# Second attention of a four-layer block on one core: choice, query projections and packing moved, scatters and gathers exchanged

## The chip, the cores and the metric

The kernel runs on one core of one Trainium2 chip (TRN2). The metric is the time on the device in microseconds (us), the median of three runs. Engines are named as in the profile: PE is TensorE (matmuls and transposes), DVE is VectorE, ACT is ScalarE, POOL is GpSimd, SP is SyncE. They run beside each other and meet at semaphores. Indirect DMAs (gathers and scatters of rows by index) are issued by POOL, one instruction for 128 rows; plain DMAs here by SP.

## The reference, cut to what matters

The input is 16 sequences of 512 tokens with 256 features, in float32. Four layers follow each other, each on a normalised input and each added to its input:

```python
x = x + attn_a(layernorm(x), ...)   # 16 heads, global and windowed
x = x + ffn(layernorm(x), ...)      # mixture of 16 experts, 4 chosen per token
x = x + attn_b(layernorm(x), ...)   # chunks of 128: local softmax + linear state, gated
x = x + ffn(layernorm(x), ...)      # the same mixture again
```

In `attn_b`, q, k, v and gate are projections of 256 to 512 features. For each chunk of 128 tokens there is a causal softmax of q k^T times v, and a `cross` term, q times the sum of k^T v over all earlier chunks; their sum is multiplied by the gate and projected back to 256 features.

The mixture routes each token: sigmoid scores, the two best of four groups, the four best experts in these; the weights are divided by their sum and scaled. `out` is the weighted sum of the chosen experts' outputs plus a shared expert.

## The kernel before

The kernel is four phases, one after the other, each with a program of its own for every engine: `phase_a` (first attention), `phase_f` (first mixture), `phase_b` (second attention, which also finishes the first mixture and begins the second), `phase_e` (second mixture). The change is in `phase_b` alone.

**How tokens move.** Per group of 4 sequences (`BATCH`), tokens are scattered by expert into a table in DRAM (`slots`), one indirect DMA for 128 tokens and one of their four choices, so 16 (`PICKS`) a sequence. The experts' outputs lie in `made`; 16 gathers a sequence bring them back to SBUF (`yg`), where DVE adds them with their weights (`combine`, line 1953). `phase_b` does, for sequences in turn: the gathers and the combine of the first mixture; the attention; the routing of the second mixture (`groups`, `choose`, `place`, `weigh`); and the scatters of all sequences but the last four into `slots`.

**The loop of `phase_b`.** `iterations` calls a `body` of every engine for s = -2 to 16. In body s the sequence s is in its attention core, sequence s+1 in the front (its transposes and projections), s+2 in combine and normalise, s-1 in routing. A body is cut into 20 slots e = 0 to 19 (`NSLOT`); each engine goes through them in order and within a slot by the order of the `if`s, and nothing but semaphores ties the engines together. So the slot numbers are an order written out by hand, engine by engine. I call "body 7" the stretch in which s = 7.

**PE's order in a body** (names as in the code): slot 0 the scores `D` (line 2338) and front transpose T0 (2315); slot 1 T1; slot 3 the first part of the cross scores O (2350); slot 4 the rest of O, the transposes of the softmax `PT` (2358), then projection q0; slot 5 the first product with v (2370), then q1; slots 6 and 7 q2, q3; slots 8 to 15 k and v in turn; 16 to 19 the gates; the routing matmuls rT0, rT1 at 6, rL at 8, rX (the ranks, 2292) at 16, each behind the front's of its slot. A projection is six matmuls of 128x512 (lines 2268 to 2270). Each front or routing result fills a PSUM bank (`BANK`) and raises the semaphore `f_done`; the engine that empties the bank raises `f_act` or `f_dve`, and `bank_free` makes PE wait for it before the bank's next use.

**The softmax** goes from D by DVE (mask and scale 2202, maximum 2207), ACT (exp 1901), DVE (2210, 2212) to PE's transposes, and ACT copies those out (1907) before the product with v may start. The transposed input leaves PSUM twice: by ACT as `xh` (1856) and by DVE as the rest `xl` (2189). A projection waits for both.

**DVE's order**: slot 0 the mask and the maximum; 2 `scaled`; 3, 4, 6, 7 `combine`; 8 to 12 statistics and normalisation; 10 `groups` (2000 to 2033); 13 the empty of v2, a residual sum, then `choose` (2038 to 2060), on which rX waits; 15 `moments`; 17 `place` and `weigh`; and at slot 18, when s is a multiple of 4, `table` (2098 to 2117) and `pack` (2126 to 2142) for the group that is now complete. `table` works out how many tiles each expert has, `pack` turns token ranks into row numbers; a scatter of that group waits for `packed`.

**POOL's order**: slots 4 to 11 the 16 gathers for sequence s+3, a pair in front of a further wait: the pair of slot e waits for `f_done` of the front's product of that slot, and for `c_step`, the combine that reads the buffer. Slot 8 also has the residual with its bias, `xres` (1821), which waits for earlier steps of DVE and for a store. Slots 12 to 19 the 16 scatters of sequence s-5 (bodies 5 to 13; body 14 has 32 of them in slots 4 to 19, body 15 the last 16). The scatters read `staged`, which SP loads behind the store of the normalised rows.

Of the kernel before, what the change touches and what calls it, by code (L numbers as in the profile page):

```python
# [5 lines left out]
P = 128  # L6
# [70 lines left out]
BATCH = 4  # L77
# [1492 lines left out]
def phase_b(nc, shared_c, routes1, routes2, base_d, made, x_out, xn_d, slots, w_gate, bias_corr, w_exp, wexp, wh, wl, woh,  # L1570
# [47 lines left out]
    MOMENT_SLOT, RLOG_SLOT, SCALE_SLOT, GROUP_SLOT, CHOOSE_SLOT, PLACE_SLOT, TABLE_SLOT = 15, 1, 2, 10, 13, 17, 18  # L1618
    RES_SLOT = 8
    GATHER_PAIRS, LAST_SLOT = range(4, 12), (9, 12, 15, 18)  # L1620
# [14 lines left out]
    with ExitStack() as ctx:  # L1635
# [88 lines left out]
        with nc.Block() as block:  # L1724
# [63 lines left out]
            def _(pool):  # L1788
# [22 lines left out]
                def body(s, par, core, front, ahead):  # L1811
                    for e in range(NSLOT):
                        if e in GATHER_PAIRS and 2 <= s + 3 < nseq:
                            i = e - GATHER_PAIRS[0]
                            pool.wait_ge(f_done, filled(s + 1, FRONT_AT[e][0]))
                            gather(s + 3, i // 2, PAIR_OF[i % 2])
# [10 lines left out]
                        if mine and front and e >= NSLOT - 2 * TB * len(mine):  # L1827
                            i = e - (NSLOT - 2 * TB * len(mine))
                            pool.wait_ge(f_done, filled(s + 1, FRONT_AT[e][0]))
                            scatter(mine[i // (2 * TB)], i // 2 % TB, PAIR_OF[i % 2])  # L1830
# [113 lines left out]
            def _(dve):  # L1944
# [151 lines left out]
                def table(n):  # L2096
# [11 lines left out]
                    step(nc.vector.tensor_scalar(jump[:], nt[:], float(P), float(REGION), ALU.mult, ALU.subtract))  # L2108
# [11 lines left out]
                def pack(n):  # L2120

                    w = slice(n * BATCH * PICKS, (n + 1) * BATCH * PICKS)
                    shape = [P, 2 * PICKS, EXPERTS - 1]
                    for i in range(2):
                        half = slice((BATCH * n + 2 * i) * PICKS, (BATCH * n + 2 * i + 2) * PICKS)
                        step(nc.vector.tensor_tensor(past, pickf[:, half].unsqueeze(2).to_broadcast(shape),
                                                     regs0[:, 1:].unsqueeze(1).to_broadcast(shape), ALU.is_ge))
                        seen()
                        step(nc.vector.tensor_tensor(past, past, jump[:, 0:EXPERTS - 1].unsqueeze(1).to_broadcast(shape), ALU.mult))
                        seen()  # L2130
                        step(nc.vector.tensor_reduce(moved[:, 2 * i * PICKS:2 * (i + 1) * PICKS], past, AX.X, ALU.add))
                        seen()
                    step(nc.vector.tensor_tensor(posi, pickf[:, w], moved[:], ALU.add))
                    seen()

                    step(nc.vector.tensor_scalar(posb, posi, 7, STEP - 1, ALU.arith_shift_right, ALU.bitwise_and))
                    step(nc.vector.tensor_scalar(posc, posi, P - 1, 2, ALU.bitwise_and, ALU.logical_shift_left))
                    seen()
                    step(nc.vector.tensor_scalar(posi, posi, -STEP * P, None, ALU.bitwise_and))
                    step(nc.vector.tensor_tensor(posc, posc, posb, ALU.add))  # L2140
                    seen()
                    nc.vector.tensor_tensor(picks[:, w], posc, posi, ALU.add).then_inc(packed, 1)
# [54 lines left out]
                def body(s, par, core, front, ahead):  # L2197
                    for e in range(NSLOT):
# [53 lines left out]
                        if s >= 1 and e == TABLE_SLOT and s % BATCH == 0:  # L2252
                            table(s // BATCH - 1)
# [587 lines left out]
```

## Time and profile before

| | us |
|---|---|
| median of 3 runs (3324.78 to 3342.89) | 3330.68 |
| the profiled execution's own time | 3329.18 |
| its span, first to last instruction | 3327.4 |
| PE busy | 2854.6 (86%) |
| DVE busy | 2212.1 (66%) |
| POOL busy | 1408.1 (42%) |
| ACT busy | 1480.5 (44%) |

The span lies 1.8 us under the profiled execution's time, and that 1.5 us under the median. In the page's strip of 40 slices `phase_b` is roughly slices 21 to 33 (from about 1738 to 2738 us). Busy time of PE is modelled from the starts of pipelined matmuls; what counts is whether PE waits, and at which clock it runs (PEclk, a share of full speed).

### The profile page before, as it was taken

How to read it: one execution, taken by the hardware profiler on the slowest of the kernel's cores; microseconds unless marked ns; L12 is line 12 of the kernel's file. 1: busy time of each engine (PE TensorE's matmuls, PEld its weight loads, DVE VectorE, ACT ScalarE, POOL GpSimd, SP SyncE). 2: the span in 40 equal slices, each digit the busy share in tenths (PEclk: the TensorE clock that was granted, in tenths of full speed). 3: DMA queues.
4: the chain of work that ended last, by engine and by line, in shares of the span. 5: the costliest groups of instructions: out<-in, count | busy, mean ns of one | idle time of the engine just before them, and what ended most of it. 6: DMA issues, size and time to landing. Idle time of an engine off the chain costs nothing. (4 is left out here: it accounts for less than half of the span.)

```text
span 3327.4 us, 59305 instructions
## 1 busy us (share of the span) xinstructions
PE 2854.6 (86%) x17728; PEld 2175.3 (65%) x17728; DVE 2212.1 (66%) x5557; ACT 1480.5 (44%) x3002; POOL 1408.1 (42%) x1606
## 2 busy tenths in 40 slices
PE   7999899899996769888979999889888938999982
PEld 4556556556564438777867777667666728788861
DVE  8878777877883867863546677657656554476653
ACT  3444455454453225555754343333333316666640
POOL 1332332332332265555125323545554524555555
PEclk9999999999997879999999999999999969999996
DMA  1121121121113246677762222333332238788874
GB/s 67 59 71 53 47 85 46 53 85 46 52 71 108 84 150 232 223 244 265 261 210 87 67 73 68 114 97 95 112 101 75 103 128 278 271 297 304 304 252 127
DMA packets 206294, 454.65 MB, mean 137 GB/s; under 512 B 28304, under 2 KB 119568, under 8 KB 204944
## 3 DMA queue, kind: packets, MB, share of 16 engines
q1 hardware_dynamic: 156816, 316.37, 27.7%
q0 software_dynamic: 49152, 134.28, 12.4%
q8 instruction: 162, 2.65, 0.3%
q14 instruction: 164, 1.34, 0.1%
HBM read 215.15 MB, written 234.88 MB: 135 GB/s over the span
## 5 line engine op out<-in xcount | busy, mean ns | idle before, releaser
L370 POOL TENSOR_SCALAR_AFFINE_SELECT a_pt<-a_pt 128x512 f32<-128x512 f32 (+1 forms) x320 | 178.9, 559 | 666.8 <-ACT a_pt L470 666.2
L470 ACT ACTIVATE a_pt<-a_S 128x384 f32<-128x384 f32 (+3 forms) x640 | 254.7, 452 | 265.4 <-PE a_S L768 262.1
L1035 POOL DMA_INDIRECT slots<-f_xn,k_picks x256 | 258.2, 1009 | 262.5 <-DVE k_picks L1378 112.8
L1793 POOL DMA_INDIRECT k_yg<-made,k_picks x224 | 225.9, 1008 | 337.0 <-DVE k_xin L1953 202.1
L2550 POOL DMA_INDIRECT f_yg<-made,k_picks x256 | 250.3, 978 | 196.9 <-issue 69.4
L618 DVE TENSOR_REDUCE a_mx<-a_FB 128x2 f32<-128x384 f32 (+4 forms) x512 | 275.8, 591 | 27.4 <-PE a_FB L743 16.2
L740 PE MATMUL a_FB<-a_kb,a_qb 128*128 128x192 bf16 (+4 forms) x1024 | 205.1, 266 | 59.5 <-DVE a_mx L618 52.0
L1807 POOL DMA_INDIRECT slots<-b_staged,k_picks x160 | 158.7, 992 | 106.6 <-issue 42.1
L781 PE MATMUL a_PV<-a_pt,a_vv 128*32 128x192 f32 (+4 forms) x2048 | 198.0, 370 | 2.7 <-POOL a_pt L377 2.6
L768 PE MATMUL a_S<-a_qs,a_ks 97*128 97x384 f32 (+3 forms) x640 | 178.4, 361 | 15.5 <-issue 15.2
L740 PEld LDWEIGHTS a_FB<-a_kb,a_qb 128*128 128x128 bf16 x1024 | 101.7, 100 | 136.3 <-DVE a_mx L618 88.2
L1524 PE MATMUL f_Z<-f_xe,f_wt 128*128 128x128 f32 x1280 | 161.4, 281 | 16.8 <-issue 9.1
L2595 ACT COPY f_wt<-f_wexp 128x512 f32 x240 | 144.8, 626 | 50.2 <-issue 26.3
L1524 PEld LDWEIGHTS f_Z<-f_xe,f_wt 128*128 128x128 f32 x1280 | 153.4, 196 | 20.1 <-issue 19.9
L2743 PE MATMUL f_Z<-f_xe,f_wt 128*128 128x128 f32 x1280 | 157.7, 277 | 5.2 <-ACT f_r L2608 4.6
L571 DVE TENSOR_SCALAR a_qb<-a_qh,a_headmask 128x512 bf16<-128x512 f32 x256 | 159.8, 691 | 0.0
L1143 ACT COPY f_wt<-f_wexp 128x512 f32 x240 | 145.1, 622 | 26.4 <-issue 23.1
L2743 PEld LDWEIGHTS f_Z<-f_xe,f_wt 128*128 128x128 f32 x1280 | 150.7, 193 | 6.6 <-issue 6.4
L2675 DVE SCALAR_TENSOR_TENSOR f_cb<-f_yg,k_wall,f_cb 128x256 f32<-128x256 f32 x256 | 123.9, 485 | 45.6 <-DMA f_yg<-made,k_picks 26.3
L2753 PE MATMUL f_Y<-f_wt,f_ge 128*128 128x256 f32 x640 | 151.5, 380 | 2.0 <-ACT f_ye L2614 1.1
L1534 PE MATMUL f_Y<-f_wt,f_ge 128*128 128x256 f32 x640 | 152.2, 381 | 1.1 <-DVE f_ye L1404 1.1
L2370 PE MATMUL b_PV<-b_st,b_v 128*128 128x512 f32 (+3 forms) x512 | 151.9, 440 | 0.9 <-ACT b_st L1907 0.9
(415 smaller groups left out, 7577.3 us busy)
## 6 DMA issues: line engine op xcount, KB each, us to landing
f_xg<-slots SPq DMA_DIRECT2D x160, 512.0 KB
made<-f_ye SPq DMA_DIRECT2D x160, 512.0 KB
slots<-a_zeros SPq DMA_DIRECT2D x16, 2560.0 KB, 9.2
a_xin<-in_x SPq DMA_DIRECT2D x16, 512.0 KB, 10.1
x_after_a<-a_xres SPq DMA_DIRECT2D x16, 512.0 KB, 2.9
f_xin<-x_after_a SPq DMA_DIRECT2D x16, 512.0 KB
f_wexp<-in_w_exp SPq DMA_DIRECT2D x8, 1024.0 KB, 13.1
bases<-f_xin SPq DMA_DIRECT2D x16, 512.0 KB, 4.5
```

Of the source, the lines that this page charges most:

```text
L370: ins = nc.gpsimd.affine_select(out=v[:, :, 0:P], in_=v[:, :, 0:P], compare_op=ALU.is_ge, fill=0.0, base=0, pattern=[[0, nh], [1, P]], cha ...
L470: nc.scalar.activation(pt[:, u % 4, b * w:(b + 1) * w], S[:, s_bank[2 * u + b], 0:w], ACT.Exp).then_inc(e_done, 1)
L571: ins = nc.vector.tensor_scalar(qb16[:, h, :], qh[:, t, :].bitcast(F32), headmask[:, h % HT:h % HT + 1], None, ALU.mult)
L618: nc.vector.tensor_reduce(mx[:, heads[0]:heads[0] + nh, qb], src[:, 0:nh * n].rearrange("p (h c) -> p h c", c=n), AX.X, ALU.max).then_inc( ...
L740: pe.matmul(o, qb16[:, h, qb * P:(qb + 1) * P], kb16[:, h // HT, k0:k0 + n], start=True, stop=(h < GLOBAL))
L768: ins = pe.matmul(S[:, s_bank[i], 0:nh * n], ks[0:ONES + 1, h // 2, kb * P:(kb + 1) * P], qs[0:ONES + 1, h:h + nh, kb * P:kb * P + n], sta ...
L781: ins = pe.matmul(PV[r:r + VW, kb * P:kb * P + n], vv[:, par, kb, h, :], pt[:, u % 4, j * n:(j + 1) * n], start=(kb == 0), stop=(kb == TB ...
L1035: nc.gpsimd.indirect_dma_start(out=slots[s // BATCH][:, :], out_offset=bass.IndirectOffsetOnAxis(ap=picks[:, i:i + 1], axis=0), in_=xn[:, ...
L1524: ins = pe.matmul(Z[:, b * P:(b + 1) * P], wt[:, v % WT, b, k * P:(k + 1) * P], xe[:, v % 2, k, b * P:(b + 1) * P], start=(k == 0), stop=( ...
L1793: nc.gpsimd.indirect_dma_start(out=yg[:, b, k, :], out_offset=None, in_=made[s // BATCH][:, :], in_offset=bass.IndirectOffsetOnAxis(ap=rou ...
L2550: nc.gpsimd.indirect_dma_start(out=yg[:, b, k, :], out_offset=None, in_=made[s // BATCH][:, :], in_offset=bass.IndirectOffsetOnAxis(ap=pic ...
L2743: ins = pe.matmul(Z[:, b * P:(b + 1) * P], wt[:, v % WT, b, k * P:(k + 1) * P], xe[:, v % 2, k, b * P:(b + 1) * P], start=(k == 0), stop=( ...
```

## The change

Five edits, all in `phase_b`:

1. `FRONT_SLOT`: T1 goes from slot 1 to slot 0, q0 from 4 to 3, q1 from 5 to 3, k, v and gates stay. On PE q0 and q1 now stand behind the first part of O and ahead of its rest and of `PT`; on ACT and DVE the emptying of T1 comes ahead of exp and of the softmax's scaling.
2. `choose` goes from slot 13 to slot 12, ahead of v2's emptying and of the residual sum.
3. `table` and `pack` are split. At slot 18 of body 4n: `jumps` (the first steps of `table`) and `pack` of one sequence. At slot 15 of body 4n+1: `pack` of one and then of two sequences. At slot 19 of that body: the rest of `table`. For the last group all of it stands at the end of body 16.
4. The scatters take slots 4 to 11, the gathers slots 12 to 19 (body 14 keeps its 32 scatters in slots 4 to 19; body 15 its order).
5. The waits that go with these: a pair now waits for the last front product up to its slot (`front_by`), a scatter for its own part of the packing.

```diff
-    FRONT_SLOT = (0, 1, 4, 5, 6, 7, 8, 9, 10, 11, 12, 13, 14, 15, 16, 17, 18, 19)
+    FRONT_SLOT = (0, 0, 3, 3, 6, 7, 8, 9, 10, 11, 12, 13, 14, 15, 16, 17, 18, 19)
+    def front_by(e):
+        return max(i for i in range(NF) if FRONT_SLOT[i] <= e)
-    ... GROUP_SLOT, CHOOSE_SLOT, PLACE_SLOT, TABLE_SLOT = 15, 1, 2, 10, 13, 17, 18
+    ... GROUP_SLOT, CHOOSE_SLOT, PLACE_SLOT, TABLE_SLOT, PACK_SLOT, REST_SLOT = 15, 1, 2, 10, 12, 17, 18, 15, 19
-    GATHER_PAIRS, LAST_SLOT = range(4, 12), (9, 12, 15, 18)
+    GATHER_PAIRS, SCATTER_AT, LAST_SLOT = range(12, 20), 4, (9, 12, 15, 18)
...
-                        pool.wait_ge(packed, s // BATCH + 1)
+                        pool.wait_ge(packed, 2 * (s // BATCH) + 1 + (s % BATCH > 0))
...
-                            pool.wait_ge(f_done, filled(s + 1, FRONT_AT[e][0]))
+                            pool.wait_ge(f_done, filled(s + 1, front_by(e)))
                             gather(s + 3, i // 2, PAIR_OF[i % 2])
...
-                        if mine and front and e >= NSLOT - 2 * TB * len(mine):
-                            i = e - (NSLOT - 2 * TB * len(mine))
+                        if mine and front and SCATTER_AT <= e < SCATTER_AT + 2 * TB * len(mine):
+                            i = e - SCATTER_AT
...
-                def table(n):
+                def jumps(n):
                     dve.wait_ge(f_dve, emptied(USE_NO[BATCH * (n + 1) - 1, "rX"]))
...
+                    step(nc.vector.tensor_scalar(jump[:], nt[:], float(P), float(REGION), ALU.mult, ALU.subtract))
+                    seen()
+
+                def table(n):
                     step(nc.vector.tensor_tensor(tmp16, tri16[:], ...))
...
-                def pack(n):
+                def pack(s, count, last=True):
+                    m = count * PICKS
+                    w = slice(s * PICKS, s * PICKS + m)
...                  # the same nine steps, on m columns, once for each call
...
                         if s >= 1 and e == TABLE_SLOT and s % BATCH == 0:
+                            jumps(s // BATCH - 1)
+                            pack(s - BATCH, 1)
+                        if s > BATCH and e == PACK_SLOT and s % BATCH == 1:
+                            pack(s - BATCH, 1, False)
+                            pack(s - BATCH + 1, 2)
+                        if s > BATCH and e == REST_SLOT and s % BATCH == 1:
                             table(s // BATCH - 1)
-                            pack(s // BATCH - 1)
+                        if s == nseq and e == NSLOT - 1:
+                            pack(s - BATCH + 1, 1, False)
+                            pack(s - BATCH + 2, 2)
+                            table(NG - 1)
```

## Rows read from the trace of the kernel before

**Rows 1.** Busy time by body: stretch, length, busy by engine, PEclk, DMA share, GB/s
```profile
1775.63:1824.93 49.30, 48.10 (x230) 37.65 (x229) 27.57 (x64) 18.71 (x39) 30.11 (x28) 1.00 0.35 105
1929.61:1981.99 52.38, 50.82 (x262) 40.33 (x261) 36.53 (x115) 20.49 (x44) 18.82 (x17) 1.00 0.24 72
2034.38:2098.40 64.02, 54.70 (x261) 42.99 (x260) 47.47 (x142) 20.58 (x44) 27.41 (x26) 0.92 0.27 86
2161.58:2224.46 62.88, 55.76 (x261) 43.30 (x260) 36.69 (x114) 20.58 (x44) 33.36 (x33) 0.92 0.31 98
2472.57:2537.10 64.53, 56.24 (x262) 43.93 (x260) 37.64 (x120) 20.53 (x44) 35.37 (x34) 0.89 0.32 101
2537.10:2596.45 59.35, 53.81 (x261) 41.26 (x260) 44.10 (x120) 19.00 (x42) 17.36 (x16) 0.97 0.17 58
2596.45:2658.02 61.57, 53.31 (x261) 41.22 (x260) 29.98 (x89) 21.04 (x44) 36.20 (x36) 0.98 0.31 109
```

**Rows 2.** PE's waits, bodies 2 to 4: total us, times, longest
```profile
PE b_PV L2292 <- issue: 3.6, 3, 1.2
```

**Rows 3.** PE's waits, bodies 6 to 11
```profile
PE b_PV L2292 <- issue: 16.7, 6, 3.3
```

**Rows 4.** Timeline, DVE, bodies 3, 7 and 0: start, length, instruction, [idle before, releaser]
```profile
1933.38 0.69 DVE L2202 SCALAR_TENSOR_TENSOR b_sm<-b_DB,b_maskc 128x512 f32<-128x512 f32 x1 [2.36 <-PE b_DB L2338]
...
2171.22 0.69 DVE L2202 SCALAR_TENSOR_TENSOR b_sm<-b_DB,b_maskc 128x512 f32<-128x512 f32 x1 [11.58 <-remote]
...
1782.67 0.69 DVE L2202 SCALAR_TENSOR_TENSOR b_sm<-b_DB,b_maskc 128x512 f32<-128x512 f32 x1 [11.74 <-remote]
```

**Rows 5.** Timeline, PE, starts of bodies 7 and 5
```profile
2161.58 3.73 PE L2338 MATMUL b_DB<-b_kT,b_qT 128*128 128x128 f32 x32
...
2175.31 1.12 PE L2358 MATMUL b_DB<-k_ident,b_sm 128*128 128x128 f32 x4 [3.12 <-DVE b_sm L2212]
...
2050.01 1.11 PE L2358 MATMUL b_DB<-k_ident,b_sm 128*128 128x128 f32 x4 [5.83 <-DVE b_sm L2212]
```

**Rows 6.** Timeline, POOL, end of body 7, start of body 8; then body 0
```profile
2211.20 1.01 POOL L1807 DMA_INDIRECT slots<-b_staged,k_picks  x1 [0.30 <-issue]
...
2218.17 0.97 POOL L1807 DMA_INDIRECT slots<-b_staged,k_picks  x1 [2.09 <-remote]
...
2232.20 0.97 POOL L1807 DMA_INDIRECT slots<-b_staged,k_picks  x1 [0.31 <-issue]
...
1779.71 0.95 POOL L1793 DMA_INDIRECT k_yg<-made,k_picks  x1 [0.30 <-issue]
```

**Rows 7.** Timeline, POOL and ACT, first mixture, with gathers, then without
```profile
1688.28 0.96 POOL L1070 DMA_INDIRECT k_yg<-made,k_picks  x1 [0.30 <-issue]
...
1690.21 0.60 ACT L1156 ACTIVATE f_r<-f_Z 128x512 f32<-128x512 f32 x1 [2.83 <-remote]
...
1708.01 0.60 ACT L1156 ACTIVATE f_r<-f_Z 128x512 f32<-128x512 f32 x1
```

**Rows 8.** Timeline, DVE, table and pack at the start of body 5
```profile
2035.71 0.17 DVE L2098 TENSOR_TENSOR b_nt<-b_cnt,k_regs 128x16 f32<-128x16 f32 x1
...
2044.84 0.22 DVE L2133 TENSOR_TENSOR b_raw<-k_pickf,b_moved 128x64 int32<-128x64 f32 x1
...
2045.93 0.68 DVE L2202 SCALAR_TENSOR_TENSOR b_sm<-b_DB,b_maskc 128x512 f32<-128x512 f32 x1
```

**Rows 9.** Timeline, POOL and DVE in body 13, then DVE in body 3
```profile
2553.52 2.44 POOL L1821 TENSOR_TENSOR b_xres<-k_xin,b_bo 128x1024 f32<-128x1024 f32 x1 [7.95 <-DVE b_rxn L1993]
...
2553.26 5.97 DVE L1953 SCALAR_TENSOR_TENSOR k_xin<-k_yg,k_wall,k_xin 128x256 f32<-128x256 f32 x8
...
1939.80 2.04 DVE L1953 SCALAR_TENSOR_TENSOR k_xin<-k_yg,k_wall,k_xin 128x256 f32<-128x256 f32 x4
```

**Rows 10.** Timeline, ACT in body 3: the softmax's transposes copied out
```profile
1939.89 0.79 ACT L1907 COPY b_st<-b_DB 128x128 f32<-128x128 f32 x4
```

**Rows 11.** Timeline, DVE, first instruction of the last phase
```profile
2739.13 0.43 DVE L2647 COPY f_wt<-f_wexp 128x512 f32 x1 [1.03 <-PEq L1724]
```

More of the change, by code:

```diff
@@ L1617, in phase_b @@
     C_SLOT = (3, 4, 6, 7)
-    MOMENT_SLOT, RLOG_SLOT, SCALE_SLOT, GROUP_SLOT, CHOOSE_SLOT, PLACE_SLOT, TABLE_SLOT = 15, 1, 2, 10, 13, 17, 18
+    MOMENT_SLOT, RLOG_SLOT, SCALE_SLOT, GROUP_SLOT, CHOOSE_SLOT, PLACE_SLOT, TABLE_SLOT, PACK_SLOT, REST_SLOT = 15, 1, 2, 10, 12, 17, 18, 15, 19
     RES_SLOT = 8
-    GATHER_PAIRS, LAST_SLOT = range(4, 12), (9, 12, 15, 18)
+    GATHER_PAIRS, SCATTER_AT, LAST_SLOT = range(12, 20), 4, (9, 12, 15, 18)
     PAIR_OF = (range(0, 2), range(2, TOP_K))
@@ L1826, in body @@
                             scatter(mine[0], LAST_SLOT.index(e), range(TOP_K))
-                        if mine and front and e >= NSLOT - 2 * TB * len(mine):
-                            i = e - (NSLOT - 2 * TB * len(mine))
-                            pool.wait_ge(f_done, filled(s + 1, FRONT_AT[e][0]))
+                        if mine and front and SCATTER_AT <= e < SCATTER_AT + 2 * TB * len(mine):
+                            i = e - SCATTER_AT
+                            pool.wait_ge(f_done, filled(s + 1, front_by(e)))
                             scatter(mine[i // (2 * TB)], i // 2 % TB, PAIR_OF[i % 2])
@@ L2118, in table @@
                                             ).then_inc(table_done, 1)
-                def pack(n):
[L2122 to L2133, printed above, removed]
+                def pack(s, count, last=True):
+                    m = count * PICKS
+                    w = slice(s * PICKS, s * PICKS + m)
+                    shape = [P, m, EXPERTS - 1]
+                    over, far = past[:, 0:m], moved[:, 0:m]
+                    pi, pb, pc = posi[:, 0:m], posb[:, 0:m], posc[:, 0:m]
+                    step(nc.vector.tensor_tensor(over, pickf[:, w].unsqueeze(2).to_broadcast(shape),
+                                                 regs0[:, 1:].unsqueeze(1).to_broadcast(shape), ALU.is_ge))
@@ L2134, in pack @@
                     seen()
-                    step(nc.vector.tensor_scalar(posb, posi, 7, STEP - 1, ALU.arith_shift_right, ALU.bitwise_and))
-                    step(nc.vector.tensor_scalar(posc, posi, P - 1, 2, ALU.bitwise_and, ALU.logical_shift_left))
+                    step(nc.vector.tensor_tensor(over, over, jump[:, 0:EXPERTS - 1].unsqueeze(1).to_broadcast(shape), ALU.mult))
                     seen()
-                    step(nc.vector.tensor_scalar(posi, posi, -STEP * P, None, ALU.bitwise_and))
@@ L2140, in pack @@
-                    step(nc.vector.tensor_tensor(posc, posc, posb, ALU.add))
+                    step(nc.vector.tensor_reduce(far, over, AX.X, ALU.add))
                     seen()
-                    nc.vector.tensor_tensor(picks[:, w], posc, posi, ALU.add).then_inc(packed, 1)
+                    step(nc.vector.tensor_tensor(pi, pickf[:, w], far, ALU.add))
+                    seen()
+                    step(nc.vector.tensor_scalar(pb, pi, 7, STEP - 1, ALU.arith_shift_right, ALU.bitwise_and))
@@ new lines, in pack @@
+                    step(nc.vector.tensor_scalar(pc, pi, P - 1, 2, ALU.bitwise_and, ALU.logical_shift_left))
+                    seen()
+                    step(nc.vector.tensor_scalar(pi, pi, -STEP * P, None, ALU.bitwise_and))
+                    step(nc.vector.tensor_tensor(pc, pc, pb, ALU.add))
+                    seen()
+                    ins = nc.vector.tensor_tensor(picks[:, w], pc, pi, ALU.add)
+                    if last:
+                        ins.then_inc(packed, 1)
+                    else:
+                        step(ins)
```

1 line of the change is left out of this document (removed).

## The prediction

> **What bounds the kernel now.** I read the page's strip first (PE busy nearly throughout `phase_b`), then the busy time by body. PE bounds the phase: in body 3 it is busy 50.82 of 52.38 us at full clock, while DVE has 36.53 and POOL 18.82 [rows 1]. There are two kinds of body. Bodies 1 to 4, which have gathers and no scatters, take 52.3 to 52.4 us each; the eight bodies 5 to 12 take 61.6 to 64.5 (62.8 in the mean), at a granted clock of 0.89 to 0.93 [rows 1]. So what is to be explained is 10 us times eight. PE's waits come next: in bodies 2 to 4 the only one of size is the ranks' matmul rX, 1.2 us a body [rows 2]; in bodies 6 to 11 it is 2.8 a body [rows 3].
>
> Then the start of a body. In body 7 PE computes D in 3.73 us, to 2165.31 [rows 5], yet DVE takes it up at 2171.22, after 11.58 us of idleness, released by "remote" [rows 4]. So the signal was 5.9 us late. In body 3 D starts at 1929.61 [rows 1], so ends near 1933.3, and DVE takes it at 1933.38 [rows 4]: no delay. What differs is on POOL. In body 7 the scatters of slots 12 to 19 can't keep up with PE: one every 0.97 + 0.31 = 1.28 us, 16 of them 20.5 us, and in slots 12 to 19 of a clean body only some 12 us are left; the last of body 7 ends at 2233.17, 8.7 us into body 8 [rows 6]. I read: while POOL issues an unbroken train of indirect DMAs, PE's completion signals reach the others late, and they come 1 to 2 us after it stops. Scatters are not needed for it. In body 0, before any scatter, the gathers of the start run to 1780.66 [rows 6]; D began at 1775.63 [rows 1], so was done near 1779.4, and DVE gets it at 1782.67 [rows 4], 3.3 us late and 2.0 after the last gather. In the first mixture the last of a run of gathers ends at 1689.24, ACT gets PE's bank at 1690.21 after 2.83 idle ("remote"), where without gathers it does not wait [rows 7].
>
> When the signal comes late, PE has only T0, T1 and the first of O, then waits (3.12 us before PT in body 7 [rows 5]), and a stretch at the lower of its two clock levels follows. Body 13, whose gathers are gone and which still starts behind body 12's train and has its own in slots 12 to 19, takes 59.35 [rows 1].
>
> **Edit 4, scatters and gathers exchanged (the main term).** The train in the last slots is the same length whichever kind it is: a gather takes 0.95 and 0.30 [rows 6], 16 make 20.0 us. From now on it stands there in each of the bodies -1 to 12, not only 5 to 13.
> - Bodies 1 to 4 (four): each now starts behind a train and ends in one, as body 13 did: 59.35 - 52.38 = +7.0 each. In body 13 another cost comes with it: `xres` is no longer held up by gathers before it; it runs for 2.44 us at 2553.52, and DVE's combines, eight in 5.97 us, stretch from the 4 in 2.04 of body 3 [rows 9] (0.75 against 0.51 each). That moves into bodies 1 to 4 also, as slots 4 to 11 are empty on POOL there; it is in the 7.0.
> - Bounds of this term. Below: nothing, if gathers hold nothing back (0). Above: 62.8 - 52.4 = 10.4 each, the difference of a body with both. I take 7.0, since body 13 has exactly one train of 16.
> - Body 0: it starts 3.3 us late behind gathers in slots 4 to 11 already [rows 4, 6]; with them in slots 12 to 19 they end later, and it also gets a train of its own at its end. Bounds 0 and 7.0; I take half, +3.5.
> - Bodies 5 to 12: 32 indirect DMAs before and after, 41 of 63 us of POOL's queue; the late train stays, only of the other kind. Scatters in slots 4 to 11 then are paced by PE's products, as gathers were in body 3, where nothing waited. 0. Bounds: -10.4 each (gathers harmless, the rival below) and +2.
> - Body 13: starts behind a train as before, its own scatters move ahead. Body 14 no longer starts behind one (61.57 before [rows 1]), but its 36 POOL instructions remain. Together -2, bounds 0 and -9.
>
> The Trainium skill ("DMA: Bandwidth & Descriptors", section "Anatomy of one DMA — SWDGE (gpsimd) path") says that a DMA's signal waits until its write is confirmed, and that this lasts longest where the write goes to HBM. A scatter writes HBM, a gather writes SBUF, so by that rule the exchange would take the heavier kind out of the critical end. Whether it holds PE's signals back is not on that page; the rows of body 0 and of the first mixture show gathers doing so. By the rule bodies 1 to 4 would cost less and bodies 5 to 12 gain, in the extreme as in rival A; by the rows neither.
>
> The page "SBUF — State Buffer" (section "SBUF: two separate sides") of the Trainium skill calls the port pair of DVE and GpSimd an exclusive lock, held for a whole instruction. That agrees with the combines beside `xres` [rows 9]; it would add to bodies 1 to 4 what the body-13 comparison already holds.
>
> **Edit 1, T1, q0 and q1 forward.** PE has six matmuls more twice, some 2.8 us, between the first O and PT. In a body whose D is late this could fill the wait before PT (3.12 [rows 5]), but the filling needs xl, which DVE writes at the start, and PT then stands behind q0 and q1 when DVE is done. After PT the first product with v must wait for ACT's copies, 0.79 us [rows 10] plus their signal, where q0 stood between them before. So +0.9 us in a clean body, and in one with a late D I take 1.2 (bounds -2.5, the wait filled, and +2). Bodies 1 to 4 and 6 to 12: eleven times 1.2 = +13.2.
>
> **Edit 2, choose one slot earlier.** It goes ahead of v2's emptying. The wait at rX, 1.2 us a clean body [rows 2] and 2.8 in the others [rows 3], should go. But v2's bank is then emptied later by the length of choose, and its next use waits for that; with a train at the end the releases come late anyway, and the wait passes to another line. I count 0 for all bodies (bounds -2.8, the wait gone and nothing in its place, and +1, a later bank).
>
> **Edit 3, table and pack split.** In body 5 both stood ahead of the mask: from 2035.71 to about 2045.9, 10.2 us [rows 8], and PE waited 5.83 us for the softmax [rows 5]. That wait goes, but what then is late is D itself: in body 7 the mask comes 9.6 us after the start, in body 5 it came 2045.93 - 2034.38 = 11.6 [rows 4, 8]. Gain 2 us in bodies 5 and 9, and 13's start, against some 10 us of packing now in slots 15 and 19 of the same bodies; DVE is busy 47.47 of 64.02 there [rows 1], so much is covered, yet v's and the gates' banks wait behind it. I call it 0, bounds -4 and +3 for each of the three. At the phase's end it is exposed: DVE alone works until 2738.11, 1.03 us before the next phase's first instruction [rows 11]. The last group is cut in three calls with nine steps each where there were twelve in all, 15 more instructions of about 0.2 us [rows 8]: +3, nothing hides it.
>
> **Edit 5, the waits.** A pair in slots 12 to 19 waits for the same product as before. The scatter of slot 4 waits for packing done a body earlier. Behind it on POOL stands `xres`, and behind that the gathers, whose first combine is in slot 3 of the next body. 0. In body -1 T1 and q0 reach for weights a little earlier: +1 (bounds 0 and 3).
>
> **Sum.** 28.0 (bodies 1 to 4) + 3.5 (body 0) - 2 + 13.2 + 3 + 1 = +46.7 on 3329.18: 3375.9. The profiled execution is 1.5 under the median, so 3377. Its own range, with 4 to 10 us for the main term and 0 to 2 for edit 1: 3350 to 3405.
>
> **Rivals.**
> A. Gathers, even in a long train, hold back nothing that matters, and scatters in slots 4 to 11 neither. For it: body 14 has scatters in slots 4 to 11 and a clock of 0.98 [rows 1]; the gathers of bodies 1 to 4 cost nothing. Against it: body 0 and the first mixture [rows 6, 7]. Then bodies 5 to 12 fall from 62.8 to about 52.8, 8 x -10 = -80; body 13 -6, body 14 -1; bodies 1 to 4 0; the tail +3; the packing +3. About -81: 3250. Chance 0.18.
> B. Gathers hold signals back half as much (1.5 to 3.3 us [rows 4, 7] against 5.9): bodies 1 to 4 4 x 3.5 = +14, body 0 +2, bodies 5 to 12 8 x -3.5 = -28, edit 1 +7, tail +3. About -2: 3329, from 3300 to 3350. Chance 0.22.
> C. As forecast, and more: packing in slots 15 and 19 delays the emptying of v and gates, and xl is not ready for q0. Decides where DVE's lead falls under 2 us. Another +2.5 in each of 14 bodies, +35: 3412. Chance 0.10.
> The forecast: 0.50.
>
> **How the numbers follow.** A measurement here can tell about 0.5% (17 us) from no change. Slower by more: the forecast nearly whole, C, and some of B: 0.58. Within 0.5%: 0.17, mostly B. Faster: A, some of B and of unseen gains from edits 2 and 3: 0.25. The range leaves out A's lower half and the top of C: 3270 to 3408; the likeliest case's own is 3350 to 3405.
>
> **What would show it.** Right: bodies 1 to 4 at 58 to 62 us, with DVE's mask released by "remote" 4 to 6 us after D's end, and gathers running 7 to 9 us into the next body; bodies 5 to 12 still over 61 at a clock of 0.9; no wait at line 2292 in bodies 1 to 4; a new wait at line 2370 for ACT's copies; the last phase beginning 3 us later after PE's last product. Wrong: the mask in body 7 taken up at D's end although a train of gathers still runs (A), or bodies 1 to 4 unchanged at 52.4. If the sum is right and bodies 5 to 12 have got shorter while others got longer by as much more, the mechanism is not the one I gave.

## The result and the profile after

The changed kernel takes 3410.15 us (median of 4 runs, 3405.24 to 3417.21), the kernel before 3328.36 (4 runs): a ratio of 1.024, 95% interval 1.0216 to 1.0265. It is 82 us slower (80 by the ratio); forecast was slower, at 3377, with a range to 3408. The profiled execution took 3405.24 us, its span is 3403.3 against 3327.4.

The stretches of six bodies in the changed kernel (length, busy time of PE, PEld, DVE, ACT and POOL with counts, granted clock, DMA share, GB/s), bodies 0, 3, 5, 7, 13 and 14, which answer to [rows 1]:

```profile
1774.36:1837.11 62.75, 50.05 (x230) 39.08 (x229) 26.17 (x64) 18.18 (x38) 21.06 (x22) 0.89 0.19 59
1959.66:2021.22 61.56, 54.24 (x262) 42.25 (x260) 38.45 (x114) 20.34 (x44) 17.71 (x18) 0.94 0.20 61
2082.98:2150.71 67.73, 55.85 (x262) 43.69 (x260) 44.50 (x144) 21.73 (x46) 35.33 (x35) 0.90 0.33 103
2213.32:2278.23 64.91, 55.51 (x262) 41.73 (x261) 36.84 (x115) 19.91 (x44) 34.20 (x34) 0.95 0.31 98
2601.71:2662.57 60.86, 54.85 (x261) 42.01 (x260) 37.59 (x116) 20.69 (x44) 25.44 (x24) 0.94 0.24 78
2662.57:2730.11 67.54, 54.81 (x261) 42.37 (x260) 34.78 (x108) 19.93 (x42) 28.33 (x27) 0.95 0.24 80
```

Body 3 went from 52.38 to 61.56 with the same work on PE. Every body length, read off in the same way from the starts of D (us):

| body | 0 | 1-4, mean | 5 | 6-12, mean | 13 | 14 | last, to phase_e |
|---|---|---|---|---|---|---|---|
| before | 49.3 | 52.4 | 64.0 | 62.7 | 59.4 | 61.6 | 81.1 |
| changed | 62.7 | 61.5 | 67.7 | 64.4 | 60.9 | 67.5 | 84.0 |
| difference, all | +13.4 | +36.4 | +3.7 | +12.3 | +1.5 | +6.0 | +2.9 |

They sum to 76.2, close to the difference of the spans (75.9). Half of it lies in bodies 1 to 4.

PE's waits in the whole phase of the changed kernel (what it waited for: us, times, longest):

```profile
PE b_Y L2289 <- DVE b_xl L2201: 45.3, 11, 11.8
PE b_PV L2289 <- ACT b_kT L1868: 25.7, 9, 3.1
PE b_Y L2336 <- issue: 20.4, 30, 1.1
PE b_PV L2391 <- ACT b_st L1911: 14.0, 16, 0.9
PE b_DB L2359 <- issue: 12.7, 18, 1.8
...
PE b_PV L2313 <- DVE b_chosen L2064: 6.9, 1, 6.9
```

The ranks' wait (31.6 us in this view of before) has gone but for the 6.9 of the last body. In its place q0 (line 2289) waits 45.3 us for `xl`, k3's bank 25.7 for ACT, and the product with v (2391) 16 times 0.87 us for ACT's copies.

Body 0 is the plainest case. The timelines of DVE, ACT, POOL and PE of the changed kernel there (start, length, instruction, idle before and releaser):

```profile
1787.13 0.69 DVE L2214 SCALAR_TENSOR_TENSOR b_sm<-b_DB,b_maskc 128x512 f32<-128x512 f32 x1 [15.73 <-remote]
```
```profile
1791.32 1.07 ACT L1860 CAST b_xh<-b_Y 128x512 fp32r<-128x512 f32 x2 [14.77 <-remote]
```
```profile
1787.69 0.95 POOL L1797 DMA_INDIRECT k_yg<-made,k_picks  x1 [0.30 <-issue]
1788.65 2.36 POOL L1825 TENSOR_TENSOR b_xres<-k_xin,b_bo 128x1024 f32<-128x1024 f32 x1
```
```profile
1774.36 3.73 PE L2359 MATMUL b_DB<-b_kT,b_qT 128*128 128x128 f32 x32
1777.93 1.04 PE L2336 MATMUL b_Y<-k_ident,b_xn 128*128 128x128 f32 x8
1778.80 2.75 PE L2371 MATMUL b_PV<-b_qT,b_kT 128*128 128x384 f32 x8
1793.38 0.77 PE L2289 MATMUL b_Y<-b_xh,b_wl 128*128 128x512 f32 x1 [11.82 <-DVE b_xl L2201]
...
1798.30 2.78 PE L2371 MATMUL b_PV<-b_qT,b_kT 128*128 128x256 f32 x16
```

PE has D ready at 1778.1 and both transposes at 1779.0. DVE gets the first 9.0 us later, while the gathers still run; ACT gets the second 12.3 us later, after the last of the gathers (1787.69). All this time POOL did nothing but start a gather every 1.26 us. And the 2.78 us of the rest of O, which before filled such a wait, stand at 1798.30, behind q0 and q1.

Body 3, POOL and PE, shows a second thing:

```profile
1960.49 0.95 POOL L1797 DMA_INDIRECT k_yg<-made,k_picks  x1 [0.30 <-issue]
1963.67 0.95 POOL L1797 DMA_INDIRECT k_yg<-made,k_picks  x1 [2.23 <-remote]
...
1969.95 0.95 POOL L1797 DMA_INDIRECT k_yg<-made,k_picks  x1 [0.30 <-issue]
```
```profile
1961.21 0.37 PE L2359 MATMUL b_DB<-b_kT,b_qT 128*128 128x128 f32 x1 [0.44 <-issue]
1962.61 0.27 PE L2359 MATMUL b_DB<-b_kT,b_qT 128*128 128x128 f32 x1 [1.03 <-issue]
...
1973.70 0.77 PE L2289 MATMUL b_Y<-b_xh,b_wl 128*128 128x512 f32 x1 [4.21 <-DVE b_xl L2201]
```

POOL's own wait for PE's last gate product, which PE finished by 1959.8, ended at 1963.67, 2.2 us after the train had stopped for it; so the train throttles itself once. And within D, a run of matmuls that wait for nobody, PE stopped three times, for 0.4 to 1.0 us.

Body 14 is long for another reason. Its signals are on time: ACT takes the front's transpose 4.2 us after the start, as in an undisturbed body. But DVE comes to the mask 6.9 us after D is done without having been idle, because the packing and the rest of the table, which edit 3 put at slots 15 and 19 of body 13, are worked off right in front of it:

```profile
2673.06 0.20 DVE L2124 TENSOR_SCALAR k_wofi<-b_et 128x80 int32<-128x80 f32 x1
2673.18 0.68 DVE L2214 SCALAR_TENSOR_TENSOR b_sm<-b_DB,b_maskc 128x512 f32<-128x512 f32 x1
```

The phase's end, DVE: the next phase starts 84.0 us after the last D, 2.9 later than before (81.1), as the forecast's 3 had it [rows 11]:

```profile
2814.14 0.43 DVE L2668 COPY f_wt<-f_wexp 128x512 f32 x1 [1.38 <-issue]
```

### The profile page after: what moved, and what is told of

Its sections match the earlier page's. It is cut to its first block and busy times, and to the rows that moved or that the text cites. A ratio compares the mean times of both kernels' runs of the same rounds, so it can differ in the third digit from the quotient of the medians.

```text
span 3403.3 us, 59365 instructions
## 1 busy us (share of the span) xinstructions
PE 2883.1 (85%) x17728; PEld 2189.5 (64%) x17728; DVE 2224.3 (65%) x5617; ACT 1480.7 (44%) x3002; POOL 1398.0 (41%) x1606
## 5 line engine op out<-in xcount | busy, mean ns | idle before, releaser
L2571 POOL DMA_INDIRECT f_yg<-made,k_picks x256 | 249.3, 974 | 195.6 <-issue 67.7
L1797 POOL DMA_INDIRECT k_yg<-made,k_picks x224 | 217.7, 972 | 245.0 <-PE b_FB L2291 159.6
L740 PE MATMUL a_FB<-a_kb,a_qb 128*128 128x192 bf16 (+4 forms) x1024 | 205.3, 266 | 59.6 <-DVE a_mx L618 52.2
## 6 DMA issues: line engine op xcount, KB each, us to landing
f_wexp<-in_w_exp SPq DMA_DIRECT2D x8, 1024.0 KB, 12.1
```

The costliest lines, as they stand in the source:

```text
L740: pe.matmul(o, qb16[:, h, qb * P:(qb + 1) * P], kb16[:, h // HT, k0:k0 + n], start=True, stop=(h < GLOBAL))
L1797: nc.gpsimd.indirect_dma_start(out=yg[:, b, k, :], out_offset=None, in_=made[s // BATCH][:, :], in_offset=bass.IndirectOffsetOnAxis(ap=rou ...
L2571: nc.gpsimd.indirect_dma_start(out=yg[:, b, k, :], out_offset=None, in_=made[s // BATCH][:, :], in_offset=bass.IndirectOffsetOnAxis(ap=pic ...
```

## The experiments

In each experiment "Measured" gives first the ratio to the kernel before, run on the same chip, with its 95% interval, and then what the kernel takes over it (the ratio less 1, times 3330 us). The profiles give a second measure, from one execution of each kernel: the length of `phase_b` from the first D to the next phase's first instruction, 963.5 us before. The rest of the program, which no run changed, took 2359.9 to 2380.6 us in these profiles, so part of a difference of whole times is not the edit's. Both, in us against before:

| | by the ratio | `phase_b` alone |
|---|---|---|
| the changed kernel | +80 | +76.3 |
| 1, the exchange alone | +36 | +31.6 |
| 2, all but the exchange | +23 | +18.1 |
| 3, the front alone | +47 | +34.1 |
| 4, choose and packing alone | -18 | -9.9 |
| 5, scatters spread | -38 | -51.2 |
| 6, thin gathers | +55 | +56.5 |
| 7, a train in mid-body | +41 | +54.6 |
| 8, the exchange, paced | +11 | +5.2 |
| 9, the changed kernel, paced | +26 | +30.4 |
| 10, without the front; with T1 alone | +36; +40 | +47.9; +43.5 |
| 11, staged rows earlier | +82 | +73.0 |
| 12, in the order of the text | -66, -22, -44, -57 | -54.6, -27.8, -54.5, -56.2 |

**1. The exchange alone** (edits 4 and 5).

```diff
-    GATHER_PAIRS, LAST_SLOT = range(4, 12), (9, 12, 15, 18)
+    GATHER_PAIRS, SCATTER_AT, LAST_SLOT = range(12, 20), 4, (9, 12, 15, 18)
```

> The kernel before with the exchange alone: scatters in slots 4 to 11, gathers in 12 to 19. Theory (a long unbroken train of indirect DMAs at the end of a body holds PE's completion signals back, whichever kind it is): bodies 1 to 4 go from 52.4 to 59-61 us, body 0 from 49 to 58-62, bodies 5 to 12 stay within 2 us of before, in all +40 to +60 us. Rival (the projections put forward are the main cost, PE now waits at q0 for xl, and the exchange alone costs little): under +25 us. Rival (gathers in a train are harmless): bodies 5 to 12 near 53, the kernel 50 us or more faster than before.

Measured: 1.0108 (1.005 to 1.0167), +36 us. Body 0 58.0, bodies 1 to 4 59.8 in the mean (+7.4 each), body 5 68.4, bodies 6 to 12 62.0 (before 62.7), body 14 57.3. The theory's body lengths came out, but for body 5 (+4.4); its total is just under what was expected. Neither rival: gathers in the last slots cost as much as scatters there, as bodies 5 to 12 hardly changed when the kinds changed places.

**2. All but the exchange.**

```diff
-    GATHER_PAIRS, SCATTER_AT, LAST_SLOT = range(12, 20), 4, (9, 12, 15, 18)
+    GATHER_PAIRS, LAST_SLOT = range(4, 12), (9, 12, 15, 18)      # scatters in 12 to 19
```

> The changed kernel with the exchange undone (gathers in slots 4 to 11, scatters in 12 to 19), all other edits kept. Theory: bodies 1 to 4 back to 52 to 53.5 us, the kernel +5 to +25 us over before. Rival (the projections put forward are the main cost): +50 us or more.

Measured: 1.007 (1.0044 to 1.0097), +23 us; bodies 1 to 4 at 52.2.

**3. T1, q0 and q1 forward, alone.**

```diff
-    FRONT_SLOT = (0, 1, 4, 5, 6, ...
+    FRONT_SLOT = (0, 0, 3, 3, 6, ...
```

> The kernel before with T1, q0 and q1 forward and nothing else. Theory: about +0.9 us in bodies 1 to 4 (PE waits 0.9 at the product with v for ACT's copy) and -1 to +2 in bodies 5 to 12, in all 0 to +20 us. Rival (main cost): +40 us or more.

Measured: 1.0142 (1.0101 to 1.0184), +47 us. The expectation failed, and the rival's number came. Bodies 1 to 4 are 53.5 (+1.1 each, as forecast), but body 0 is +7.4, bodies 5 to 12 +2.6 each and body 14 +5.4. PE's waits in bodies 5 to 11 of this kernel:

```profile
PE b_PV L2296 <- issue: 20.4, 7, 4.0
PE b_Y L2272 <- DVE b_xl L2193: 20.3, 6, 7.1
...
PE b_PV L2374 <- ACT b_st L1911: 2.6, 3, 0.9
```

Line 2272 is q0's. Before, PE waited 12.1 us in these bodies for the softmax ahead of PT, and never at q0. In body 7 the rest of O changed its place; first the kernel before, where all of O is done ahead of PT's wait [rows 5], then this one:

```profile
2166.03 4.69 PE L2350 MATMUL b_PV<-b_qT,b_kT 128*128 128x384 f32 x17
2171.16 1.04 PE L2350 MATMUL b_PV<-b_qT,b_kT 128*128 128x128 f32 x7 [0.44 <-issue]
```
```profile
2195.73 0.77 PE L2272 MATMUL b_Y<-b_xh,b_wl 128*128 128x512 f32 x1 [3.09 <-DVE b_xl L2193]
...
2200.12 2.78 PE L2354 MATMUL b_PV<-b_qT,b_kT 128*128 128x256 f32 x16
```

**4. Choose and packing, alone** (edits 2 and 3).

> The kernel before with choose at slot 12 and table and pack split, nothing else. From the two kernels with the front moved (+43 us with it alone, +24 with these two added) they are worth -19 us. If they add up: -15 to -25 us against before, with bodies 1 to 4 at 51 to 51.5 us. Rival (they only help behind the moved projections): within 5 us of before.

Measured: 0.9945 (0.9925 to 0.9964), -18 us, inside the expectation (-10 in `phase_b` of its one profile). Bodies 1 to 4 are 51.04 (the ranks' 1.2 us and a little more), and body 5 falls from 64.0 to 52.1, at full clock:

```profile
2036.14:2088.23 52.09, 51.02 (x261) 40.23 (x260) 39.18 (x127) 19.09 (x42) 24.49 (x24) 1.00 0.31 90
```

Bodies 6 to 12 gained nothing (62.9): there PE itself now stops again and again within D, 60 times and 41.0 us in the phase, with waits for nothing that the profile shows.

**5. Scatters spread.** The same 32 indirect DMAs in a body, in another place.

```diff
+    SINGLE = (5, 7, 9, 11) + tuple(range(12, 20))
+                        old = SCATTERS.get(s - 1, ())
+                        if len(old) == 1 and front and e < 4:
+                            pool.wait_ge(f_done, filled(s + 1, front_by(e)))
+                            scatter(old[0], TB - 1, (e,))
+                        if len(mine) == 1 and front and e in SINGLE:
+                            ...
+                            scatter(mine[0], i // TOP_K, (i % TOP_K,))
```

> The kernel before with the scatters of bodies 5 to 13 spread so that no long train forms: one each in slots 5, 7, 9, 11 and 12 to 19, the last four in slots 0 to 3 of the next body; the gathers stay. The same 32 indirect DMAs a body. Theory (the unbroken train is what costs): bodies 5 to 12 from 62.8 to 53-57 us, in all -50 to -80 us. Rival (the mere number of indirect DMAs or their traffic costs the 10 us a body): bodies 5 to 12 stay over 61, in all within 10 us of before.

Measured: 0.9885 (0.984 to 0.9931), -38 us. Bodies 6 to 12 fall from 62.7 to 57.1 in the mean, three of them to 55.8. Body 7, against 62.88 at a clock of 0.92 [rows 1]:

```profile
2153.02:2208.86 55.84, 52.38 (x261) 41.39 (x260) 36.59 (x114) 20.48 (x44) 34.14 (x34) 0.97 0.36 113
```

In bodies 6 to 12, all but 9, DVE takes the mask up at D's end again. Body 5 stays at 64.7: there the block of table and packing ahead of the mask takes over. The number of indirect DMAs is not what costs.

**6. Thin gathers.** The exchange alone, with an eighth of the bytes.

```diff
-                            out=yg[:, b, k, :], out_offset=None, ...
+                            out=yg[:, b, k, 0:32], out_offset=None, ...
```

> The kernel with the exchange alone, but each gather of this phase brings 32 of the 256 numbers of a row (the rest of the combine reads what lay there). As many gathers, an eighth of their bytes. If POOL's issuing of the train holds the signals: bodies 1 to 4 stay at 59 to 60 us. If the traffic of the train does: they fall to 52 to 55 us.

Measured: 1.0164 (1.0131 to 1.0197) on a chip where the kernel before took 3351; bodies 1 to 4 at 60.7, where the full gathers gave 59.8. Body 3 of each, first thin, then full:

```profile
1957.69:2019.22 61.53, 55.37 (x262) 42.84 (x261) 38.19 (x114) 20.05 (x44) 18.21 (x18) 0.94 0.11 30
```
```profile
1946.31:2006.11 59.80, 54.01 (x261) 42.30 (x260) 38.32 (x114) 20.15 (x44) 17.95 (x18) 0.94 0.21 62
```

30 GB/s against 62, and no gain. It is not the bytes. (The kernel leaves seven eighths of each gathered row out.)

**7. A train in the middle of the body.** The kernel before, with the gathers of bodies 1 to 4 unbroken from slot 8 on.

```diff
+                        if e == GATHER_PAIRS[4] and 1 <= s <= 4:
+                            pool.wait_ge(f_done, filled(s + 1, FRONT_AT[e][0]))
+                            for i in range(2 * TB):
+                                gather(s + 3, i // 2, PAIR_OF[i % 2])
```

> The kernel before, with the 16 gathers of bodies 1 to 4 in one unbroken train from slot 8 on, where they stood in pairs in slots 4 to 11; nothing is at the end of the body. Theory (the unbroken train costs, wherever it stands): signals of PE in slots 9 to 16 come over 2 us late and bodies 1 to 4 go from 52.4 to 55-60 us. Rival (only a train over the start of the next body costs, since D is short of cover there): under 53.5 us.

Measured: 1.0123 (1.0089 to 1.0156), +41 us; bodies 1 to 4 at 61.8 to 64.7, more than either side expected, though D's signal is on time there. POOL and ACT in body 3:

```profile
1982.86 0.96 POOL L1797 DMA_INDIRECT k_yg<-made,k_picks  x1 [39.59 <-PE b_FB L2278]
...
2001.83 0.95 POOL L1797 DMA_INDIRECT k_yg<-made,k_picks  x1 [0.30 <-issue]
2002.80 2.35 POOL L1829 TENSOR_TENSOR b_xres<-k_xin,b_bo 128x1024 f32<-128x1024 f32 x1
```
```profile
2005.67 0.69 ACT L1872 ACTIVATE b_kT<-b_FB,b_bk 128x512 f32<-128x512 f32 x1 [13.97 <-remote]
```

PE had finished this product of k by 1992.7. ACT stood 13.97 us for it, 12.9 of them in vain, and was let go 2.9 us after the last of 16 gathers. The two products before, done 4.3 and 7.1 us into the train, were taken at once; the one done 8.5 us into it reached DVE 6.6 us late. The first 7 us of this train held nothing back. But a train costs wherever it lies.

**8. The same gathers with pauses.** The exchange alone, each pair of bodies 1 to 4 waiting until the pair before has landed.

```diff
+                            if i and 1 <= s <= 4:
+                                j = i - 1
+                                pool.wait_ge(gathered[j // 2], 16 * (TOP_K * (s + 1) + 2 * (j % 2 + 1)))
                             gather(s + 3, i // 2, PAIR_OF[i % 2])
```

> The kernel with the exchange alone, but in bodies 1 to 4 each pair of gathers waits until the pair before it has landed. The same 16 gathers stand in the same slots and end even later, with a pause after each pair. Theory (the unbroken train holds the signals, they come in its pauses): bodies 1 to 4 from 59.8 to 52.5 to 56 us. Rival (gathers over the start of the next body cost whatever their spacing): 59 us or more.

Measured: 1.0032 (1.0017 to 1.0047), +11 us, 25 less than without the pauses. Body 1 and body 3, then POOL at the start of body 3, then DVE's mask in body 3, here and in the exchange alone:

```profile
1829.61:1891.81 62.20, 55.59 (x262) 42.31 (x261) 36.80 (x109) 21.40 (x45) 14.72 (x14) 0.92 0.16 49
1942.99:1994.85 51.86, 50.80 (x262) 40.33 (x261) 36.04 (x115) 20.30 (x44) 18.98 (x19) 1.00 0.24 72
```
```profile
1952.16 0.98 POOL L1797 DMA_INDIRECT k_yg<-made,k_picks  x1 [2.53 <-issue]
1953.44 1.06 POOL L1797 DMA_INDIRECT k_yg<-made,k_picks  x1 [0.30 <-issue]
1958.13 0.95 POOL L1797 DMA_INDIRECT k_yg<-made,k_picks  x1 [3.63 <-issue]
...
1964.07 1.16 POOL L1797 DMA_INDIRECT k_yg<-made,k_picks  x1 [0.30 <-DVE k_xin L1960]
```
```profile
1946.76 0.69 DVE L2209 SCALAR_TENSOR_TENSOR b_sm<-b_DB,b_maskc 128x512 f32<-128x512 f32 x1 [2.37 <-PE b_DB L2345]
```
```profile
1957.37 0.69 DVE L2206 SCALAR_TENSOR_TENSOR b_sm<-b_DB,b_maskc 128x512 f32<-128x512 f32 x1 [5.84 <-remote]
```

The gathers now reach 22 us into body 3, where in the exchange alone they ended 11 us into it. With the pauses the mask starts 3.77 us after D's start, at its end; without them 11.06 us after it, 5.3 late, and D itself took 5.7 us where it takes 3.73. Bodies 2 to 4 take 51.2 to 51.9 us at full clock, less than before the change. Body 1, behind body 0's unbroken train, is still 62.2. This is the clearest of the runs. The wait for a landing is what made the pauses; pauses of another kind were not tried.

**9. The changed kernel with those pauses** in bodies -1 to 4.

> The changed kernel, but in bodies -1 to 4 each pair of gathers waits until the pair before has landed. Theory: signals are no longer late in bodies 0 to 4; body 0 from 62.7 to 50-55, bodies 1 to 4 from 61.5 to 52-54 us, in all 35 to 50 us under the changed kernel. If the longer gathers delay the combines and with them the body, or the front costs there by itself: less than 25 us.

Measured: 1.0079 (1.0061 to 1.0097), +26 us, 54 less than the changed kernel. Body 0 55.7, bodies 1 to 4 52.2, bodies 5 to 14 as in the changed kernel. The waits of PE in bodies 2 to 4 are then

```profile
PE b_PV L2394 <- ACT b_st L1914: 2.6, 3, 0.9
PE b_FB L2325 <- ACT b_qT L1871: 1.0, 3, 0.3
```

**10. The changed kernel without the front edit, and with T1's part of it alone.**

```diff
-    FRONT_SLOT = (0, 0, 3, 3, 6, ...
+    FRONT_SLOT = (0, 1, 4, 5, 6, ...    # the first kernel
+    FRONT_SLOT = (0, 0, 4, 5, 6, ...    # the second
```

> The changed kernel with T1, q0 and q1 back in slots 1, 4 and 5. Alone, the exchange cost +34, choose and packing -17, the front +43: +60, where the change measured +81. If the 21 left over belong to the front behind trains (every body then has late signals, and PE waits at q0 for xl): about +15 to +25 us over before, bodies 1 to 4 at 59 to 60. If choose and packing bring nothing behind trains: about +35 to +45 us.

> The changed kernel with only q0 and q1 back in slots 4 and 5, T1 stays in slot 0. If putting q0 and q1 ahead of the softmax's transposes is what costs: as without the whole front edit, within 10 us of it. If T1 beside the scores costs (emptied ahead of exp and of the scaling): near the changed kernel, +60 us or more over before.

Measured: 1.0107 (1.0073 to 1.0142), +36 us, and 1.0119 (1.01 to 1.0137), +40. The first is the exchange's own +36: behind trains, choose and the split packing bring nothing that these ratios can show, and the front makes the rest, 44 (28 in `phase_b`). The second: q0 and q1 cost about 40 (33 in `phase_b`); the 4 us between the two kernels, of opposite sign in `phase_b`, are within the noise, so no cost of T1 is shown. In one place the split packing costs plainly: body 14, 57.3 us in the exchange alone with the mask at D's end, is 65.0 here with the mask 6.9 us late.

**11. Staged rows loaded earlier.** In body 7 of the changed kernel POOL waited long for the rows to be scattered:

```profile
2237.52 1.00 POOL L1811 DMA_INDIRECT slots<-b_staged,k_picks  x1 [14.07 <-DMA b_staged<-normalised]
```

```diff
+                    for i in early:        # ahead of sp.wait_ge(r_done, s)
+                        stage(i)
```

> The changed kernel, but SP loads the rows to be scattered ahead of its wait for the routing's normalised rows. There POOL stood still until 24 us into body 7 for this load, 14 us, before its first scatter. If that late start lengthens the train at the end of the body: scatters start 10 us earlier, the gathers' train shortens by 3 to 8 gathers, bodies 6 to 12 fall from 64.4 by 2 to 6 us each, in all 15 to 40 us under the changed kernel. If the train is limited by the short slots 12 to 19 alone (16 gathers of 1.27 us against 12 us of PE): bodies 6 to 12 within 1 us of the changed kernel.

Measured: 1.0246 (1.0217 to 1.0275), the changed kernel's number. The first scatter of body 7 still starts at 2237.21, now with

```profile
2237.21 1.01 POOL L1818 DMA_INDIRECT slots<-b_staged,k_picks  x1 [9.14 <-PE b_Y L2298]
```

So it waited for at least two things that come together; removing the one that the profile had named gained nothing.

**12. Towards a better kernel.** Spread scatters with edits 2 and 3; the same with the front edit; with the rest of the table in slot 5 of body 4n+2; with four more scatters moved to slots 0 to 3.

> The spread scatters (one each in slots 5, 7, 9, 11, 12 to 19, four in the next body) on the kernel before, with two edits of the change added: choose at slot 12, and table and pack split. Theory: bodies 5, 9 and 13, 64.7, 61.4 and 56.9 us with the spread alone, fall to 54 to 57 as the block of table and pack ahead of the mask is gone; bodies 1 to 4 lose the 1.2 us at the ranks; in all 50 to 75 us faster than before. Rival (the packing in slots 15 and 19 now delays v and the gates by as much): within 10 us of the spread alone, which was 46 us faster than before.

> The kernel with scatters spread, choose at slot 12 and the packing split, with T1, q0 and q1 forward as well. Moved alone on the kernel before they cost 43 us, 7 in body 0 and about 2.5 each in bodies 5 to 12. If most of that is from late signals (PE waits at q0 for xl): here +0.5 to +1.5 a body, in all +8 to +25 us over the same kernel without it (51 us or so faster than before at the most). If it costs by itself: +40 us or more.

> The kernel with scatters spread, choose at slot 12 and the packing split, with the rest of the table moved from slot 19 of body 4n+1 to slot 5 of body 4n+2. There PE waited 5 us for the softmax in bodies 10 and 14 (64.1 and 64.3 us). If the table ahead of the mask caused that: those fall to 55 to 59 us and body 6 from 58.3 to 55, in all 5 to 17 us under that kernel. If not: no difference beyond the spread of a few us.

> The kernel with scatters spread, choose at slot 12 and the packing split, with four scatters more taken out of slots 12 to 19 (one in every second slot) and put in pairs into slots 0 to 3 of the next body. If the train over the end of the body is still what lifts bodies 6 to 12 (54 to 58 us against 51 in bodies 1 to 4): 1 to 3 us less each, 5 to 20 us in all. If the signals only move to be late in slots 0 to 4: no better, or up to 15 us worse.

Measured: 0.9802 (0.9774 to 0.9829), 66 us under before, 3282.33 us. It has the best ratio, but the kernel before took 3351 in the same set of runs; by the time alone it is no faster than the spread scatters by themselves (3282.38), and in `phase_b` 3 us faster. What edits 2 and 3 add to the spread is therefore not settled: they take 8.5, 7.4 and 5.8 us out of bodies 5, 9 and 13, while bodies 10 and 14 and the last stretch are 8.2, 7.5 and 9.6 longer. With the front edit 0.9934 (0.9911 to 0.9957), 44 more by the ratios, where 8 to 25 were expected. It ran on the same chip in a later set of runs, in which the kernel before took 3329; by the times alone it is 25 more, and in `phase_b` 27, so the size is nearer the expectation than the ratios say. Bodies 1 to 4 are again +1.1 each, bodies 6 to 12 +1.9. The table moved: 0.9869 (0.9845 to 0.9893), 3285.61 us; body 14 fell from 64.3 to 60.5, but body 10 stayed at 63.4 us. Four more scatters moved: 0.9828 (0.9804 to 0.9851), 3276.59 us, no better. So four kernels (run 5 among them) end within 9 us of each other by their times, and which is the best is not shown.

The traces say in part what lifts single bodies (10 and 14, 61 to 65 us) in these kernels. In the first of them DVE comes to the mask 7.5 and 7.2 us late there without having been idle, with packing and the table's rest in front of it, as in body 14 above; with the table moved it is 2.0 and 3.2 us late. In body 14 that fits what was gained. In body 10 it is not the whole: PE then waits up to 4.4 us for ACT at the transposes for the routing and 3.3 at one of k's banks, and why was not tested.

## Why the prediction failed, step by step

- **The train holds PE's signals back** (the mechanism): right, and shown. Runs 7 and 8 made it and took it away (+9 to +12 us a body, and -8), and run 6 took out the bytes as its cause. Its signs came: no wait at the ranks' matmul in bodies 1 to 4, a new one of 0.87 us at the product with v, gathers 11 us into the next body (7 to 9 forecast), the mask 2.7 to 4.0 us late in bodies 1 to 4 (4 to 6 forecast) behind a D stretched to 6.4 to 9.2 us.
- **Edit 4**: right in its large terms. Bodies 1 to 4: 28.0 forecast, 29.6 in the exchange alone. Bodies 5 to 12: 0 forecast, -0.6 in all. Bodies 13 and 14: -2, measured -4.0. Body 0: +3.5 forecast, +8.7 measured, over its upper bound of 7.0: body -1 has no attention in it, its last slots pass quickly, and the train reached 14 to 15 us into body 0. The term summed to +29.5 and the exchange measured +36 (17 to 56).
- **Edit 1**: this is the step that failed: "So +0.9 us in a clean body, and in one with a late D I take 1.2 (bounds -2.5, the wait filled, and +2)", in sum +13.2. It measured +47 alone and 44 in the changed kernel by the ratios, 34 and 28 by `phase_b` alone: more than twice the term by either. The clean bodies were right (+1.1). In the bodies with late signals it was +2.6 (run 3, bodies 5 to 12), and bodies 0, 5, 13 and 14, which the sum left out altogether, were +7.4, +3.0, -0.9 and +5.4. What I missed is the cover: the rest of O (16 matmuls, 2.78 us) needs no late signal, and before it ran while PE waited for the softmax; q0, which needs the late `xl`, was put in front of it. PE then stands at q0 with work behind it. Its 2.78 us are about the +2.6 that a body lost. The forecast counted what the moved instructions add and what idle time they could fill, not what they block. The runs show the wait at q0, and run 10 that q0 and q1, not T1, are the cost; that it is O's cover in particular is read from the timelines, not from a run that moves O alone.
- **Edit 2**: 0 was right here. Alone it gains the ranks' 1.2 us in clean bodies; the changed kernel has no clean ones, and its PE waits 25.7 us for k3's bank instead, as forecast.
- **Edit 3**: 0 within the phase came out of two things that the forecast did not have apart. In body 5 12 us were gained alone (run 4), and behind trains 4.6 (run 10 against run 1), since D itself is late there, the reason given. But the work was not hidden where it went: in body 14 it stands ahead of the mask, and the body is 7.7 us longer (65.0 against 57.3 in the exchange alone). That term is missing from the sum. At the end of the phase +3 was forecast; DVE's own work there, from the table's first step to its last, went from 10.3 to 12.6 us, +2.3. That the whole last stretch shows +2.9 is in part luck, as it varied from 74.5 to 85.9 us between kernels that left this work alone.
- **Where the sum fell short**: by bodies some 30 us, namely 10 in body 0, 9.5 in bodies 13 and 14, 7.6 in bodies 5 to 12 and 3.6 in bodies 1 to 4. The large term, bodies 1 to 4, was nearly right; what was missing lay mostly in bodies to which the forecast gave little or nothing.
- **Rivals**: A (gathers harmless) and B (half as harmful) fell with the exchange alone. C's number, 3412, was nearly met, mostly by luck: `xl` was indeed late for q0, which C named second, but packing cost at the mask of body 14 (its wait for DVE at v's bank there is 1.2 us), and the excess was not 2.5 us in each of 14 bodies. The range's top, 3408, was 2 us too low.
- **The Trainium skill** ("DMA: Bandwidth & Descriptors", "Anatomy of one DMA — SWDGE (gpsimd) path") has the completion slowest for writes to HBM. By that rule bodies 5 to 12 should have gained by the exchange; they stayed at 62.8 (run 1), so the measurement bears out no such difference here. What the page "SBUF — State Buffer" (section "SBUF: two separate sides") says of the lock between DVE and GpSimd agrees with the combines beside `xres` (0.75 us each against 0.51 [rows 9]), but no run here tells it apart from the rest.

## What to carry to other kernels

Look at how densely POOL issues indirect DMAs, not at how many there are: a pause of 2.5 to 3.6 us after each pair made 16 of them free, and without pauses they cost 7 to 12 us a body wherever they stood. Keep work that needs no fresh signal ahead of work that does, since that is what fills a late signal's wait; and when instructions are moved forward, price what they are put in front of. An edit's worth depends on which bound stands next: choose and packing gained 18 us alone (10 in `phase_b`) and nothing that could be shown behind the trains. And work split off to a later slot has to be followed to what stands behind it there.

## What the runs showed of the hardware

- While POOL issued indirect DMAs every 1.26 to 1.28 us, PE's completions reached ACT and DVE up to 12 to 13 us late (12.3 in body 0 of the changed kernel, 12.9 in run 7). They mostly arrived 1 to 3 us after the train's last one, but D's in bodies 0 and 2 to 4 of the changed kernel came while it still ran. In run 7 the products done in the first 7 us of the train came on time. Bytes made no difference (30 against 62 GB/s); pauses of 2.5 to 3.6 us removed it (the mask 0.04 us after D's end in bodies 2 to 4 of run 8). Why the signals are held is not shown.
- PE itself stopped in runs of matmuls that wait for nothing, for up to 1.8 us at a time: 12.7 us in D and 20.4 in the transposes over the phase in the changed kernel, 41.0 in D in run 4, and 1.4 and 7.4 before. Why is not shown.
- The granted clock was 1.00 in bodies 1 to 4 before, and 0.89 to 0.97 in bodies 0 to 14 of the changed kernel. A single late signal need not lower it: body 0 before, with D's 3.3 us late, stayed at 1.00. After a long wait (11.82 us in body 0, 4.21 in body 3 of the changed kernel) PE ran a stretch at its lower level (1.2 GHz), where a projection's matmuls came every 0.43 us instead of 0.23.
